# Attention and FP4 feed-forward on eight cores: PSUM copies moved to ScalarE, the softmax bound split up and moved, the quantizer rewritten

## What is computed

```python
xn = _layernorm(x)                       # x: (4, 4096, 1024)
q  = (xn @ Wq.T)                         # 8 heads of 256
kv = xn @ Wkv_down.T                     # latent, 64 wide
k  = kv @ Wk_up.T ; v = kv @ Wv_up.T
attn = softmax(q k^T / 16) v @ Wo.T
h  = silu(fp4(xn) @ fp4(Wg).T) * (fp4(xn) @ fp4(Wu).T)      # 2816 wide
out = x + attn + fp4(h) @ fp4(Wd).T
```

## Time and profile before

| | us |
|---|---|
| median of three runs | 5168.04 |
| fastest, slowest run | 5121.86, 5291.51 |
| profiled execution | 5120.92 |
| its span on the slowest core | 5119.1 |
| PE busy in it | 2578.2 (50%) |
| VectorE busy | 3195.7 (62%) |
| ScalarE busy | 768.0 (15%) |
| POOL busy | 105.5 (2%) |

### The profile page before, as it was taken

The page is one execution under the profiler, slowest core; times in us unless marked ns, Lnnn a source line. Parts: engine busy times, 40 slices in busy tenths (PEclk is TensorE's granted clock), DMA queues, the critical chain, the costliest instruction groups (busy, mean ns, idle before and its releaser), DMA issues. The chain is left out here.

```text
span 5119.1 us, 36562 instructions; the slowest of 8 cores (5096.4 to 5119.1 us)
## 1 busy us (share of the span) xinstructions
PE 2578.2 (50%) x9840; PEld 951.0 (19%) x9840; DVE 3195.7 (62%) x5377; ACT 768.0 (15%) x1155; POOL 105.5 (2%) x197
## 2 busy tenths in 40 slices
PE   1111154493958678493958677743342333333335
PEld 0101122120212112120212122321120111111112
DVE  7777756487584949577585844306653662663665
ACT  0000000150513324150514233000000000000000
POOL 0000000000000000000000000000000000000000
PEclk9999997595968879595968778676675667667667
DMA  1101121010000101000000102270024006005001
GB/s 35 32 25 33 52 44 26 9 32 19 22 29 13 37 5 35 13 29 20 21 25 15 31 9 40 67 166 11 0 62 72 0 0 133 0 0 117 17 0 58
DMA packets 195843, 173.61 MB, mean 34 GB/s; under 512 B 147136, under 2 KB 157632, under 8 KB 193600
## 3 DMA queue, kind: packets, MB, share of 16 engines
q1 hardware_dynamic: 179680, 144.86, 11.4%
q0 software_dynamic: 15968, 26.42, 2.1%
HBM read 98.89 MB, written 46.66 MB: 28 GB/s over the span
## 5 line engine op out<-in xcount | busy, mean ns | idle before, releaser
L640 ACT ACTIVATE pbuf<-psA,negB_col 128x512 bf16<-128x512 f32 x512 | 351.8, 687 | 1474.3 <-PE psA L626 1474.3
L640 ACT ACTIVATE pbuf<-psB,negB_col 128x512 bf16<-128x512 f32 x512 | 351.6, 687 | 287.5 <-PE psB L626 286.6
L626 PE MATMUL psA<-qT_all,kT_h 128*128 128x512 bf16 x1024 | 316.4, 391 | 0.4 <-DVEq L600 0.4
L656 PE MATMUL psC<-pbuf,V_h 128*128 128x512 bf16 x1024 | 310.1, 385 | 10.7 <-ACT pbuf L640 10.7
L626 PE MATMUL psB<-qT_all,kT_h 128*128 128x512 bf16 x1024 | 313.9, 389 | 0.0
L656 PE MATMUL psD<-pbuf,V_h 128*128 128x512 bf16 x1024 | 304.5, 379 | 12.6 <-ACT pbuf L640 12.6
L888 PE MATMUL psB<-ident_t,hq_t 128*128 128x128 f32 x176 | 48.3, 425 | 448.3 <-DVE hq_t L219 446.9
L873 DVE TENSOR_TENSOR h_t<-gs_c,psC 128x512 f32<-128x512 f32 (+1 forms) x48 | 30.9, 643 | 388.9 <-ACT gs_c L869 388.9
L888 PE MATMUL psA<-ident_t,hq_t 128*128 128x128 f32 x176 | 48.3, 425 | 445.6 <-DVE hq_t L219 444.1
L525 PE MATMUL psA<-kvT_b,wkuh 64*128 64x512 bf16 x64 | 35.9, 560 | 442.9 <-DVE kT_h L528 349.4
L676 DVE CAST o_all<-psC 128x512 bf16<-128x512 f32 x32 | 20.6, 685 | 351.9 <-PE psE L656 351.9
(11 more groups left out here) (171 smaller groups left out, 4975.2 us busy)
## 6 DMA issues: line engine op xcount, KB each, us to landing
xbuf<-x_tok SPq DMA_DIRECT2D x16, 1024.0 KB, 6.3
rbuf<-resid_scr SPq DMA_DIRECT2D x32, 512.0 KB, 5.5
wbuf<-Wg SPq DMA_DIRECT2D x44, 256.0 KB, 2.8
wbuf<-Wu SPq DMA_DIRECT2D x44, 256.0 KB, 2.7
wbuf<-Wd SPq DMA_DIRECT2D x40, 256.0 KB, 2.7
xt_buf<-xT_own SPq DMA_DIRECT2D x8, 1024.0 KB, 9.0
resid_scr<-rstage SPq DMA_DIRECT2D x8, 1024.0 KB, 6.1
resid_scr<-obuf SPq DMA_DIRECT2D x16, 512.0 KB, 3.7
```

What stands on the lines that cost most here:

```text
L626: ins = (lambda e, h=h, qq=qq, kc=kc, m=m, pb=pb: e.matmul(pb[:, :], kT_h[:, m, kc * 128:(kc + 1) * 128], qT_all[:, 2 * h + m, qq * 512:(q ...
L640: eb.em('scalar', lambda e, cglob=cglob, pb=pb: e.activation(out=pbuf[:, cglob % 2, :], in_=pb[:, :], func=AF.Exp, bias=negB_col[:], scale ...
L656: ins = (lambda e, kc=kc, cg=cg, lo=lo, hi=hi, dstp=dstp, dsl=dsl: e.matmul(dstp[dsl, 0:512], V_h[:, kc, lo:hi], pbuf[:, cg % 2, :], start ...
```

## The change

It has four parts.

1. PSUM copies go from VectorE to ScalarE: xnT and stage_q, kvT_b, qT_all, kT_h and V_h, o_all and srowq, hqT_b. `srowq` has one slot instead of two.
2. `emit_quant` has seven scratch tiles instead of four. Compares that were fused with an add are separate operations without a drain between them, and the sign is multiplied into the scale early.
3. The q part of the bound is worked out once, at the end of stage 2, for all heads, with psE and psF in turn. Eight slices over kvT_b are worked out there as well (into bt1[7], which nothing reads).
4. The k part of the bound runs in eight groups inside the preparation of a head: after each four V copies ScalarE squares a slice of kT_h, PE sums it into one of four banks, VectorE takes the maximum.

```diff
     def emit_quant(eb, F, src, dst, PL):
...
         eb.em(v, D_)
         eb.em(v, lambda e: e.tensor_reduce(out=pbm[:, 0:NB], in_=src3, axis=AX.X, op=ALU.max, apply_absolute_value=True))
+        eb.em(v, lambda e: e.scalar_tensor_tensor(out=pA[:, 0:F], in0=src, scalar=-1.0, in1=src, op0=ALU.mult, op1=ALU.max))
+        eb.em(v, lambda e: e.tensor_scalar(out=pK[:, 0:F], in0=src, scalar1=0.0, scalar2=2.0, op0=ALU.is_ge, op1=ALU.mult))
         eb.em(v, D_)
...
+        eb.em(v, lambda e: e.tensor_tensor(out=K3, in0=K3, in1=sb_, op=ALU.mult))
+        eb.em(v, D_)
...
         eb.em(v, lambda e: e.tensor_single_scalar(out=pC[:, 0:F], in_=pA[:, 0:F], scalar=0.25, op=ALU.is_gt))
+        eb.em(v, lambda e: e.tensor_single_scalar(out=pD[:, 0:F], in_=pA[:, 0:F], scalar=0.75, op=ALU.is_gt))
+        eb.em(v, lambda e: e.tensor_single_scalar(out=pE[:, 0:F], in_=pA[:, 0:F], scalar=1.25, op=ALU.is_gt))
+        eb.em(v, lambda e: e.tensor_single_scalar(out=pF[:, 0:F], in_=pA[:, 0:F], scalar=1.75, op=ALU.is_gt))
+        eb.em(v, lambda e: e.tensor_scalar(out=pG[:, 0:F], in0=pA[:, 0:F], scalar1=5.0, scalar2=2.0, op0=ALU.is_gt, op1=ALU.mult))
         eb.em(v, D_)
-        eb.em(v, lambda e: e.scalar_tensor_tensor(out=pC[:, 0:F], in0=pA[:, 0:F], scalar=0.75, in1=pC[:, 0:F], op0=ALU.is_gt, op1=ALU.add))
+        eb.em(v, lambda e: e.tensor_tensor(out=pC[:, 0:F], in0=pC[:, 0:F], in1=pD[:, 0:F], op=ALU.add))
+        eb.em(v, lambda e: e.tensor_tensor(out=pE[:, 0:F], in0=pE[:, 0:F], in1=pF[:, 0:F], op=ALU.add))
+        eb.em(v, lambda e: e.scalar_tensor_tensor(out=pG[:, 0:F], in0=pA[:, 0:F], scalar=3.5, in1=pG[:, 0:F], op0=ALU.is_gt, op1=ALU.add))
         eb.em(v, D_)
-        eb.em(v, lambda e: e.scalar_tensor_tensor(out=pC[:, 0:F], in0=pA[:, 0:F], scalar=1.25, in1=pC[:, 0:F], op0=ALU.is_gt, op1=ALU.add))
...
-            eb.wait('vector', S['tr'], S['tr'].n)
+            eb.wait('scalar', S['tr'], S['tr'].n)
...
-            eb.em('vector', lambda e, dst=dst, src=src: e.tensor_copy(dst, src).then_inc(S['trev'].h, 1))
+            eb.em('scalar', lambda e, dst=dst, src=src: e.copy(dst, src).then_inc(S['trev'].h, 1))
...
+    eb.wait('vector', S['kvev'], S['kvev'].n)
+    eb.wait('vector', S['qpj'], S['qpj'].n)
...
+    for h2 in range(NH):
+        for n in range(4):
+            for m in range(2):
+                qsl = qT_all[:, 2 * h2 + m, n * 512:(n + 1) * 512]
...
+            eb.wait('tensor', S['bnd'], S['bnd'].n)
+            eb.wait('tensor', S['pbev'], S['pbev'].n - 1)
+            pse = PSR[n % 2]
...
+            eb.wait('vector', S['bnd'], S['bnd'].n)
+            eb.em('vector', lambda e, pse=pse: e.tensor_reduce(out=bt1[:, 0:1], in_=pse[0:1, 0:512], axis=AX.X, op=ALU.max))
...
+        emit_prep(range(16))
+        NB4 = [psC0, psC1, psD0, psD1]
+        if h > 0:
+            eb.wait('tensor', S['oev'], 4 * h)
+        mmp_tgt = [0] * 8
+        for grp in range(8):
+            emit_prep(range(16 + 4 * grp, 16 + 4 * grp + 4))
+            if grp >= 1:
+                eb.wait('scalar', S['bnd'], mmp_tgt[grp - 1])
...
+                eb.em('scalar', lambda e, grp=grp, m=m: e.activation(
+                    out=sqv_t[:, m * 512:(m + 1) * 512], in_=kT_h[:, m, grp * 512:(grp + 1) * 512],
+                    func=AF.Square).then_inc(S['sco'].h, 1))
+            pse = NB4[grp % 4]
+            if grp >= 4:
+                eb.wait('tensor', S['pbev'], S['pbev'].n - 3)
...
-            eb.wait('vector', S['avq'], S['avq'].n)
-            if qglob >= 2:
-                DS['ssq'].wait_for(eb, 'vector', qglob - 2)
+            eb.wait('scalar', S['avq'], S['avq'].n)
+            if qglob >= 1:
+                DS['ssq'].wait_for(eb, 'scalar', qglob - 1)
```

More of the change, by code:

```diff
@@ L423, in build_program @@
                 eb.em('tensor', ins)
-        eb.wait('vector', S['kv_pe'], S['kv_pe'].n)
+        eb.wait('scalar', S['kv_pe'], S['kv_pe'].n)
         S['kvev'].n += 1
-        eb.em('vector', lambda e, n=n, pb=pb: e.tensor_copy(kvT_b[:, n * 512:(n + 1) * 512], pb[0:LR, 0:512]).then_inc(S['kvev'].h, 1))
+        eb.em('scalar', lambda e, n=n, pb=pb: e.copy(kvT_b[:, n * 512:(n + 1) * 512], pb[0:LR, 0:512]).then_inc(S['kvev'].h, 1))
     if debug:
@@ L456, in build_program @@
                         eb.em('tensor', ins)
-                eb.wait('vector', S['q_pe'], S['q_pe'].n)
+                eb.wait('scalar', S['q_pe'], S['q_pe'].n)
                 S['qpj'].n += 1
-                eb.em('vector', lambda e, m=m, n=n, pb=pb: e.tensor_copy(
+                eb.em('scalar', lambda e, m=m, n=n, pb=pb: e.copy(
                     qT_all[:, m, n * 512:(n + 1) * 512], pb[:, :]).then_inc(S['qpj'].h, 1))
@@ L464, in build_program @@
         eb.em('sync', lambda e: e.dma_start(out=dbg['qT'], in_=qT_all[:]).then_inc(S['out'].h, 16))
+    eb.wait('vector', S['kvev'], S['kvev'].n)
+    eb.wait('vector', S['qpj'], S['qpj'].n)
+    eb.wait('tensor', S['prep'], S['prep'].n)
+    PSR = [psE, psF]
+    for sl in range(8):
+        S['bnd'].n += 1
+        eb.em('vector', lambda e, sl=sl: e.tensor_tensor(
+            out=sqb2[0:LR, 0, :], in0=kvT_b[:, sl * 512:(sl + 1) * 512],
+            in1=kvT_b[:, sl * 512:(sl + 1) * 512], op=ALU.mult))
+        eb.em('vector', lambda e: e.drain().then_inc(S['bnd'].h, 1))
+        eb.wait('tensor', S['bnd'], S['bnd'].n)
+        if sl >= 2:
+            eb.wait('tensor', S['pbev'], S['pbev'].n - 1)
+        pse = PSR[sl % 2]
+        S['bnd'].n += 1
+        eb.em('tensor', lambda e, pse=pse: e.matmul(pse[0:1, 0:512], ones_b128[0:LR, 0:1], sqb2[0:LR, 0, :],
+                                                    start=True, stop=True).then_inc(S['bnd'].h, 1))
+        eb.wait('vector', S['bnd'], S['bnd'].n)
+        eb.em('vector', lambda e, pse=pse: e.tensor_reduce(out=bt1[:, 0:1], in_=pse[0:1, 0:512], axis=AX.X, op=ALU.max))
+        eb.em('vector', lambda e: e.drain())
+        S['pbev'].n += 1
+        if sl == 0:
+            eb.em('vector', lambda e: e.tensor_single_scalar(out=bt1[:, 7:8], in_=bt1[:, 0:1], scalar=1.0, op=ALU.mult))
+        else:
+            eb.em('vector', lambda e: e.tensor_single_scalar(out=bt1[:, 7:8], in_=bt1[:, 0:1], scalar=bt1[:, 7:8], op=ALU.max))
+        eb.em('vector', lambda e: e.drain().then_inc(S['pbev'].h, 1))
@@ new lines, in emit_prep @@
+        def emit_prep(rng):
+            for idx in rng:
+                pb = SBK[idx % 2]
+                if idx >= 2:
+                    eb.wait('tensor', S['kvev'], kv_base + idx - 1)
+                if idx < 16:
+                    m, n = idx // 8, idx % 8
+                    ins = (lambda e, h=h, m=m, n=n, pb=pb: e.matmul(
+                        pb[:, :], wkuh[:, h % 2, m * 128:(m + 1) * 128],
+                        kvT_b[:, n * 512:(n + 1) * 512], start=True, stop=True))
+                    ev = (lambda e, m=m, n=n, pb=pb: e.copy(
+                        kT_h[:, m, n * 512:(n + 1) * 512], pb[:, :]))
+                else:
+                    mt = idx - 16
+                    ins = (lambda e, h=h, mt=mt, pb=pb: e.matmul(
+                        pb[0:128, 0:256], kvT_b[:, mt * 128:(mt + 1) * 128],
+                        wvuh[:, h % 2, :], start=True, stop=True))
+                    ev = (lambda e, mt=mt, pb=pb: e.copy(V_h[:, mt, 0:256], pb[0:128, 0:256]))
+                S['prep'].n += 1
+                eb.em('tensor', lambda e, ins=ins: ins(e).then_inc(S['prep'].h, 1))
+                eb.wait('scalar', S['prep'], S['prep'].n)
+                S['kvev'].n += 1
+                eb.em('scalar', lambda e, ev=ev: ev(e).then_inc(S['kvev'].h, 1))
```

169 lines of the change are left out of this document (77 added, 92 removed).

## The result

The changed kernel takes 4723.24 us, the median of ten runs (4686.74 to 4841.92), against 5136.62 for the kernel before on the same chips (ten runs, 5116.20 to 5291.51). The ratio is 0.9173, with a 95% interval of 0.9136 to 0.9211: faster by 8.3%. The profiled execution took 4710.24 us, its span is 4708.7; that of before took 5120.92. Forecast were 4753 us (4700 to 4860) and a ratio of 0.928.

What follows compares the result with a forecast made beforehand. Attention alternates between stretches PE fills and stretches where PE waits for VectorE; VectorE carries stage 1. Stage 1 -111, stage 2 +127, attention -430, FFN +46 sum to -368 from 5120.92: 4753 us, range 4700 to 4860.

Steps and rivals of the forecast that it cites:

- The quantizer: Quantizing on VectorE: three more compares, four fewer drains; +1.21 us at 1024 columns, +0.41 at 512, +0.22 at 384.
- FFN: Longer quantizing on the path of every FFN row tile, 32 x (1.21 + 0.22) = +46 us; moved copies gain nothing.
- Rival C: Quantizing: the dropped drains return nothing, so each costs 0.62 us more than counted; 4855 us, chance 0.05.
- Stage 1: Copies on ScalarE spare VectorE's waits (-86 and -47 us), quantizing +19, weight blocks +3; sum -111 us.
- Stage 2: q's bound moved here 104 us, eight latent slices 20, with weight blocks +127; first head's preparation -18.
- Attention: Gaps between heads fall from 118.2 to 55 us, -443 over seven; 24 quarter ends inside heads cost +31.
- the group: One of eight in a head's preparation: sum matmuls, V copies and squares, 4.6 us each, 36.8 together.
- pairs of kT copies: Between heads: eight loops of copy, signal, matmul and signal, 1.44 us each, 11.5 together.
- fifth group: Between heads: PE gets there after 32 us, VectorE is free at 28, so no wait, 3 us to spare.
- A: Between heads, VectorE's four blocks stand behind the quarter's end; PE stands 12 us, seven times; 4837 us, chance 0.17.
- B: Between heads ScalarE's loops are slower: pairs 1.6 us, groups 5.2, copies 0.69; 4804 us, chance 0.15.
- D: ScalarE reloads its table 320 times, 410 us at 1.28 each: 5163 us, or slower at dearer loads; chance 0.02.

## Why the prediction was right

The time came out at 4710 in the profiled run, 43 us under the forecast, by the mechanism that was forecast. Its steps in order:

**The quantizer, +1.21, +0.41, +0.22.** Measured +1.14 at 1024 columns, +0.37 at 512 (10.75 for 10.38) and +0.14 at 384. The first two are good; the last was taken from the difference of two large terms (three operations against four drains), and such a difference carries the error of both. In the FFN this makes 32 x (1.14 + 0.14) = +41 for +46, and the piece shows +32. That figure is the lowest of seven: the six other runs with the new quantizer and ScalarE's copies in the FFN have 1608 to 1619 us there, +36 to +47. So the forecast term is too large by some 5 us, and the rest of its miss is not told apart from the differences between executions. The drains do give time back. VectorE's timeline in the first stage of the changed kernel has the new compares one behind the other, and a drain only ahead of the last row:

```profile
93.98 0.69 DVE L208 TENSOR_SCALAR PL1pF<-PL1pA 128x1024 f32<-128x1024 f32 x1
94.59 0.69 DVE L209 TENSOR_SCALAR PL1pG<-PL1pA 128x1024 f32<-128x1024 f32 x1
95.35 1.22 DVE L211 TENSOR_TENSOR PL1pC<-PL1pC,PL1pD 128x1024 f32<-128x1024 f32 x1
```

It is 0.61 us from start to start without a drain and 0.76 with one, as in the earlier trace rows. Rival C is out. The Trainium skill ("VectorE: DVE Perf Modes", section The DRAIN you can't avoid) says that chaining operations without semaphores does not skip the flush. That is no statement on a `drain` instruction between operations, which is what the change leaves out and what these rows price at 0.15 us, so the rival had read the rule further than it goes.

**Stage 1, -111.** -109.4. The tile of the other half takes 4.79 us (4.86 less the overlap) and the square root fits behind the copies, because a copy takes 0.59 and not VectorE's 0.68. A tile is 2.98 us shorter; the forecast has 2.91 us in one place and counts with 2.95 in another, which changes the sum by 1 us. The run of before with the new quantizer alone gives the two parts: +21.8 for the quantizer and its blocks (19 + 3 were forecast), so -131 for the copies (-133). With the old quantizer in both kernels the copies give -129 (703.1 to 574.5).

**Stage 2, +127 and -18.** +104.7 for +109. The q slice is 3.25 us on average, 3.24 forecast; the eight latent slices are 19.5 by the run without them (20).

**Attention, -443 and +31.** The gap fell from 118.2 to 50.9 and not to 55, so -471, and a quarter cost 0.95 and not 1.3 us, +23; together -448, as measured. The term that was mis-sized is the group, 4.24 for 4.6 us: the copy loop of half a tile is shorter than I put together from prices of single steps (8 x 0.36 = 2.9 of the 4 us). The rest of the chain stood: copies 0.59 (0.60), pairs of kT copies 1.41 (1.44), VectorE free 27.5 us behind PE's end (28), fifth group due at 32.2 (32). Head to head is 220 to 222 us, 226 forecast.

**The rivals.** A fell, with 4.7 us between VectorE's first maximum and the group that needs it, and two runs showed its price when it does come: 92 and 98 us in the attention. B fell with 4.24 us a group. D fell: the table is loaded once at the head of stage 2, as before, at 586.25 for 1.28 us, and squares and copies follow each other on ScalarE without a load between them. The list of the Trainium skill ("ScalarE: Activation LUTs", section Table sets: the hidden batching unit) that I had set beside it names copy among the functions of every set and not square; in these traces the missing name has no price.

**How good the number is.** 4710 lies at the lower end of the range of 4700 to 4860. The misses of the pieces (+2, -4, -36 and -14 us) nearly all have one sign, so they did not cancel, and they are misses of size: the waits and overlaps that the sum rests on are in the traces.

**What I had not seen** though the sum came out: that VectorE was behind PE by a little more in every quarter, before the change. I took its blocks as four to be waited for at the head's end. The sum was spared by starting from the measured gap of 118.2 us, which has the lag in it. The copies that went to ScalarE took away the lag as well, and two of the three runs that cost clearly more than expected (the quarter's copies back on VectorE, the quantizer alone) are those in which it counts.

## What to carry to other kernels

An in-order engine with filler work has a period, and it is compared with the period of the engine beside it before anything else: at 45 us against 42 the filler is no filler, and the next dependent step pays all of the lag at once. Where such an engine is held, look at the queue that frees its buffers: putting the stores ahead of the quarter rather than behind it gave room for two more blocks a head and took 177 us out of two other stages; with the stores behind the quarter the same move was worth 79 us in all. And a step that is moved out of a loop gains only if something lies beside it in its new place: q's bound cost the same 3.2 us a slice in either, and 1.9 us a head once the projections lay beside it.
